# Expert products of split operands in float32r, with the weights split during attention

## What is computed

```python
logits = xf @ Wr / temp
topw, topi = jax.lax.top_k(logits, TOP_K)
topw = jax.nn.softmax(topw, axis=-1)
for e in range(NUM_EXPERTS):
    h = xf @ W1[e] + b1[e]
    a, g = jnp.split(h, 2, axis=-1)
    y = a * jax.nn.silu(g) @ W2[e] + b2[e]
    we = jnp.sum(jnp.where(topi == e, topw, 0.0), axis=-1, keepdims=True)
    out = out + y * we
```

## Time and profile before

| | us |
|---|---|
| median of 3 runs (1123.76 to 1127.93) | 1125.69 |
| the profiled execution | 1125.17 |
| its span, first to last instruction | 1123.4 |
| PE busy | 1019.9 |
| DVE busy | 763.6 |
| ACT busy | 502.1 |
| POOL busy | 409.1 |

### The profile page before, as it was taken

One profiled execution on the slowest core, in us unless ns is written; L12 is line 12 of the kernel. 1 busy time (PEld: TensorE's weight loads), 2 busy tenths in 40 slices (PEclk: granted clock), 3 DMA queues, 4 the chain that ended last, 5 costly groups with the idle time before them and its releaser, 6 DMA issues.

```text
span 1123.4 us, 19233 instructions
## 1 busy us (share of the span) xinstructions
PE 1019.9 (91%) x5236; PEld 525.9 (47%) x5237; DVE 763.6 (68%) x2270; ACT 502.1 (45%) x1060; POOL 409.1 (36%) x777
## 2 busy tenths in 40 slices
PE   5998999999999999999895533999999999999994
PEld 2443233333333333333544531666666666666663
DVE  3776989899999999999464741555555555555552
ACT  2553177777777777777354430221222222222221
POOL 5665333333333333333252673222222222222222
PEclk9998599999999999999897656999999999999998
DMA  2769855556555444417567992222222222323222
GB/s 91 250 220 282 156 124 125 124 127 131 130 131 130 94 95 95 89 42 174 127 205 173 306 310 89 37 45 44 48 47 47 45 44 42 47 47 47 44 45 24
DMA packets 104058, 125.66 MB, mean 112 GB/s; under 512 B 26480, under 2 KB 82416, under 8 KB 103984
## 3 DMA queue, kind: packets, MB, share of 16 engines
q1 hardware_dynamic: 90688, 107.01, 38.5%
q0 software_dynamic: 13296, 17.77, 9.6%
HBM read 74.47 MB, written 49.89 MB: 111 GB/s over the span
## 4 chain that ended last, share of the span: by engine, by line
PE 80%; DVE 6%; POOL 5%; DMA 4%; issue 3%; ACT 2%; SPq 0%; POOLq 0%; DVEq 0%; ACTq 0%
PE bank L1757 22%; PE bank L791 12%; PE bank L812 12%; PE bank L773 12%; PE bank L1774 11%; POOL slot_rows L1169 3%; PE bank L1765 3%; DVE a_xn L314 2%; PE a_ckv L363 1%; PE bank L1745 1%; DVE bank L701 1%; DMA c_heads<-ctx_cols 1%; PE a_k_ps L379 1%; PE bank L1486 1%; DVE b_neg_max L704 1%
## 5 line engine op out<-in xcount | busy, mean ns | idle before, releaser
L747 ACT ACTIVATE b_prob<-bank 128x512 f32<-128x512 f32 (+3 forms) x768 | 311.9, 509 | 79.5 <-PE bank L791 78.6
L773 PE MATMUL bank<-b_k_st,b_q_st 96*128 96x512 bf16 (+3 forms) x768 | 255.5, 346 | 5.8 <-DVE b_neg_max L701 1.7
L1757 PE MATMUL bank<-w_sb,e_rowsT 128*128 x568 | 256.9, 595 | 0.4 <-issue 0.4
L701 DVE CUSTOM_DVE_ANT_0 bank<-bank,b_mask_max 128x256 f32<-128x256 f32 (+3 forms) x512 | 241.5, 508 | 22.9 <-PE bank L773 22.8
L657 POOL TENSOR_SCALAR_AFFINE_SELECT b_prob<-b_prob 128x128 f32<-128x128 f32 x512 | 149.2, 300 | 295.1 <-ACT b_prob L747 290.6
L791 PE MATMUL bank<-b_q_st,b_k_st 99*128 99x512 bf16 (+3 forms) x768 | 242.9, 333 | 4.1 <-ACT b_prob L747 2.0
L1650 POOL DMA_INDIRECT out_dram<-e_y,e_token x71 | 110.5, 1556 | 319.4 <-DVE e_y L1704 294.0
L704 DVE TENSOR_REDUCE b_neg_max<-bank 128x1 f32<-128x512 f32 x256 | 175.7, 686 | 13.7 <-PE bank L773 11.1
L1757 PEld LDWEIGHTS bank<-w_sb,e_rowsT 128*128 128x128 f32 x568 | 102.9, 191 | 103.5 <-issue 103.5
L812 PE MATMUL bank<-b_prob,b_v_aug 128*32 128x512 f32 (+3 forms) x1536 | 146.3, 500 | 0.0
L1774 PE MATMUL bank<-w_sb,e_hiddenT 128*128 x568 | 134.4, 379 | 1.8 <-ACT e_hiddenT L1727 1.8
(11 more groups left out here) (166 smaller groups left out, 886.6 us busy)
## 6 DMA issues: line engine op xcount, KB each, us to landing
w_sb<-in_L_ffn_W SPq DMA_DIRECT2D x12, 1024.0 KB, 5.2
e_rows<-slot_rows SPq DMA_DIRECT2D x72, 129.0 KB, 2.1
ctx_cols<-b_ctx_out SPq DMA_DIRECT2D x16, 512.0 KB
q_parts<-a_part_q SPq DMA_DIRECT2D x8, 768.0 KB, 4.1
k_parts<-a_part_k SPq DMA_DIRECT2D x8, 768.0 KB, 4.8
b_q_st<-q_parts SPq DMA_DIRECT2D x16, 384.0 KB, 4.9
b_k_st<-k_parts SPq DMA_DIRECT2D x16, 384.0 KB, 8.1
a_x<-in_L_attn_x SPq DMA_DIRECT2D x8, 512.0 KB, 5.1
```

The source lines that it names most:

```text
L701: nc.vector.tensor_tensor_reduce(scores, scores, mask_max[:, HALF - width:HALF], -1.0, -MASKED, ALU.add, ALU.min, to).then_inc(max_done, 1)
L747: nc.scalar.activation(prob[n % NP][:, 0:width], prob_ps[n % NS][:, 0:width], ACT.Exp, scale=SCALE).then_inc(prob_ok, 1)
L773: nc.tensor.matmul(out[:, 0:width], q_st[g % RING][0:STACK, h, i * P:(i + 1) * P], k_st[g % RING][0:STACK, h, half * HALF:half * HALF + wi ...
L1757: last = nc.tensor.matmul(out_ps[:], rowsT[c % 2][:, d * P:(d + 1) * P], w1_sb[:, bass.ds(expert, 1), d, first:first + FF].rearrange("p e ...
```

## The change

Each operand of the expert products is written as a high part, rounded to float32r, and a remainder, also float32r. A product becomes three: high by high, high by low, low by high.

- **Weights.** `Weights` holds a ring of 4 slots, each with both parts of one expert's up and down weights (24 KB a partition). During attention SP loads one expert's raw weights (1.5 MB) at `g` = 1, 2, 4, 6, 7, 9, 10, 12, in the order 3, 4, 5, 6, 7, 2, 0, 1. POOL splits each in 12 pieces of 256 columns, a cast and a subtraction a piece, at most one piece a unit. SP stores the parts of the first five (3 MB each) to DRAM at `g` = 4, 6, 8, 9, 11. Experts 2, 0 and 1 stay in SBUF; expert 3 is loaded back in `Route.sync`, in place of the down weights; 4 to 7 are loaded by SP in the expert stage, the up weights when the expert that had the slot has finished its up products, the down weights behind them.
- **Rows and hidden rows.** ACT takes the high part from PSUM (`rows_high`, `hidden_high`), DVE subtracts it for the rest (`rows_rest`, `hidden_rest`).
- **Other moves.** The multiplication by the router's weight goes from DVE to ACT. The load of a tile's rows goes from SP to ACT, behind that multiplication. The second bias is added one step later (`biased`, tile n-3), so there are three steps after the last tile.
- **Adds.** POOL waits for the add two tiles back, and for the last one only where the expert changes (`fresh`, a table that DVE makes), so two adds can be in flight.
- The memory moves follow, and POOL clears `pad_row` when the last context is stored.

```diff
@@ attention, SP @@
-            if 1 <= g <= EXPERTS:
-                sp.dma_start(w1_sb[:, g - 1, :, :], w1[g - 1].rearrange("(c p) n -> p c n", p=P)).then_inc(
-                    loaded, 16)
...
+            if g in W_STORE_AT:
+                weights.store(sp, W_STORE_AT.index(g))
+            if g in W_LOAD_AT:
+                weights.load(sp, W_LOAD_AT.index(g))
@@ attention, POOL @@
+            weights.split_at(pool, unit)
@@ class Weights @@
+    def split(self, pool, k, piece):
...
+        self.nc.gpsimd.tensor_copy(self.ring[:, n, 0, cols], self.raw[:, n, 1, cols]).then_inc(self.high_ok, 1)
+        pool.wait_ge(self.high_ok, k * PIECES + piece + 1)
+        self.nc.gpsimd.tensor_tensor(self.ring[:, n, 1, cols], self.raw[:, n, 1, cols],
+                                     self.ring[:, n, 0, cols].bitcast(F32), ALU.subtract).then_inc(self.split_ok, 1)
@@ experts, SP @@
+        for e in range(W_RING, EXPERTS):
...
+            sp.wait_ge(a_ok, done(e) + 1)
+            weights.load_parts(sp, e, 0)
+            if e == EXPERTS - 1:
...
+                sp.wait_ge(y_ps_ok, done(W_RING) + 1)
+                weights.load_parts(sp, W_RING, 1)
+            sp.wait_ge(weights.parts_in[0], 32 * (e - W_RING + 2))
+            sp.sem_inc(w1_ready, 1)
@@ experts, POOL @@
-            pool.wait_ge(added, (n + 1) * 16)
-            pool.sem_inc(landed, 1)
...
+                pool.wait_ge(added[c % 2], cycle(n, c, 0, 2) * 16)
...
+                pool.wait_ge(added[(c - 1) % 2], cycle(n, c, 1, 2) * 16 + fresh)
@@ experts, ACT @@
+        def load(n, c):
+
+            act.wait_ge(y_ok, n + 1)
...
+            act.dma_start(rows[c % B][:], dram["rows"][bass.ds(row, P), :]).then_inc(rows_ok[c % B], 16)
...
         def step(n, c, value):
+            if value is None or 2 <= n < SLOT_TILES + 2:
+                hidden_high(n - 2, c - 2)
+            if value is None or n + 1 < SLOT_TILES:
+                rows_high(n + 1, c + 1)
+            if value is None or 3 <= n < SLOT_TILES + 3:
+                weighted(n - 3, c - 3)
+            if value is None or n + AHEAD < TABLE:
+                load(n + AHEAD, c + AHEAD)
             if value is None or n < SLOT_TILES:
                 silu(n, c)
-            if value is None or 1 <= n <= SLOT_TILES:
-                hidden_turned(n - 1, c - 1)
@@ experts, PE, up @@
-                    last = nc.tensor.matmul(out_ps[:], rowsT[c % 2][:, d * P:(d + 1) * P],
...
+                    nc.tensor.matmul(out_ps[:], x_hi[:, chunk], moving(slot, 0, at, FF), start=(d == 0), stop=False)
+                    nc.tensor.matmul(out_ps[:], x_hi[:, chunk], moving(slot, 1, at, FF), start=False, stop=False)
+                    last = nc.tensor.matmul(out_ps[:], x_lo[:, chunk], moving(slot, 0, at, FF), start=False,
+                                            stop=(d == DC - 1))
```

More of the change, by code:

```diff
@@ L14 @@
 F32 = mybir.dt.float32
+F32R = mybir.dt.float32r
 BF16 = mybir.dt.bfloat16
@@ L36 @@
 FC = FF // P
-FC_EARLY = 1
 PARTS = 3
@@ L501, in index_of, with attention_phase @@
     return unit // 2 * 2 * QUAD + 2 * h + unit % 2
-def attention_phase(nc, block, life, dram, stacks, projected, room, banks, route, w1, w1_sb, w2, w2_early, loaded):
+def attention_phase(nc, block, life, dram, stacks, projected, room, banks, route, weights):
     NM, NS = 4, 3
@@ L1099, in sync @@
         self.store_x2(sp, 2)
-        for f in range(1, FC):
-            load_w2(f)
+        for layer in range(2):
+            self.weights.load_parts(sp, W_STAGES, layer)
         sp.wait_ge(self.pad_row_ok, 1)
@@ L1555, in tensor, with expert_phase @@
                     self.project(pe, 3, t)
-def expert_phase(nc, block, life, route, dram, room, banks, weights, out):
+def expert_phase(nc, block, life, route, weights, dram, room, banks, bias, loaded, out):
     def sb(name, shape, dt=F32):
@@ L1661, in _ @@
                 add(it * U + c, c)
+        for n in range(2):
+            pool.wait_ge(added[n], (SLOT_TILES - n + 1) // 2 * 16)
     @block.vector
@@ new lines, in build @@
+        weights = Weights(nc, life, low, dram, w1, w2)
+        after = Room(nc, low.next, HIGH)
+        attention = Room(nc, LOW + W_STAGES * 2 * W_COLS * BYTES[F32], HIGH)
+        end = attention.next + ATTENTION_BYTES
+        loaded = life.enter_context(nc.semaphore("loaded"))
+        block = life.enter_context(nc.Block())
+        upper = Room(nc, HIGH - STACKS_BYTES, HIGH)
+        stacks = Stacks(nc, life, upper, dram)
+        freed = Room(nc, upper.first["b_mask_max"], upper.first["b_v_aug0"])
@@ new lines, in build @@
+        over_stacks = Room(nc, upper.first["b_v_aug0"], upper.first["b_ident"])
+        bias = [over_stacks("m_b1", [P, EXPERTS, 2 * FF]), over_stacks("m_b2", [P, EXPERTS, D])]
+        second_row = over_stacks.beside("m_b1", "c_second_row1", [P, BT, ROW])
+        early = Room(nc, end, HIGH - STACKS_BYTES)
+        projected = project_phase(nc, block, life, dram, stacks, Room(nc, LOW, end), x, w_dkv, w_uk, w_uv, w_uq)
+        banks = [life.enter_context(nc.psum_tensor(f"bank{n}", [P, HALF], F32)) for n in range(8)]
@@ new lines, in build @@
+        route = Route(nc, life, early, freed, after, bias, banks, dram, x, w_o, w_r, temp, (b1, b2), weights,
+                      loaded, second_row, out)
+        attention_phase(nc, block, life, dram, stacks, projected, attention, banks, route, weights)
+        assert attention.next <= end and after.next <= end
+        block.sync(route.sync)
+        block.gpsimd(route.gpsimd)
+        block.vector(route.vector)
+        block.scalar(route.scalar)
+        block.tensor(route.tensor)
+        room = Room(nc, upper.first["b_mask_max"], upper.first["b_v_aug0"])
@@ L1841 @@
+        expert_phase(nc, block, life, route, weights, dram, room, banks, bias, loaded, out)
 _INS = ["L0_attn_x", "L0_attn_W_DKV", "L0_attn_W_UK", "L0_attn_W_UV", "L0_attn_W_UQ", "L0_attn_W_O", "L0_ffn_Wr",
```

305 lines of the change are left out of this document (192 added, 113 removed).

## The result

The changed kernel takes **1108.06 us** in the median of 4 runs (1104.23 to 1109.71), the kernel before 1125.87 beside it (1123.76 to 1127.93). The ratio is 0.984, with a 95% interval of 0.9823 to 0.9857. It is faster by 1.6%, clear of the scatter and in the direction of the forecast, but by 18 us where 57 were forecast, and 1108 lies above the range. The profiled execution took 1107.14 us with a span of 1105.4, against 1125.2 and 1123.4 of before.

A forecast was written before the change was run, and what follows sets the result against it. The prediction took PE to bound the expert stage at 5.82 us a step, with the row load's loop next. From 1125.2: -74 for steps, +10 weight loads, +6 attention, +1 tail and start, giving 1068 us; range 1033 to 1105.

The forecast's parts named there:

- d: Expert stage: stationary loads of float32r not hidden at each of 24 products; step 7.1 us, time 1224 us; chance 0.09.
- e: Expert stage: float32r streams at two periods a column; step 8.4 us, time 1315 us; chance 0.05.
- the loop of the row load: Expert stage: row load's loop over two steps, 4.48 plus 5.08 us, sets 4.78 us a step; gain 74 us.
- Reading the expert's number: Expert stage: PE's read of the number between row transposes and products, 0.36 us, taken from the gap at the first tile.
- The products, 0.216 and 0.109: Expert stage: float32r products of 512 and 256 columns at one period a column; PE alone 4.56 us a step.
- rival (b): Expert stage: PE stays the bound at 4.56 us a step, transfers hidden; 1037 us; chance 0.18.
- Rival (c): Transfers cost their upper bounds or the row-load loop is 5.0 us a step; 1093 us; chance 0.17.
- Weight loads in the stage: Expert stage: 12 MB for experts 4 to 7 slows row loads, 9 x 1.1, 10 us; bounds nothing and 27.
- Attention: Attention: SP's queue with the weight stores makes maximum rows late by some 2 us, three times; +6 us, bounds 0 and 15.
- POOL's splits: Attention: 96 pairs of cast and subtraction, 1.2 us each, covered by POOL's waiting; nothing, or 5 to 15 us uncovered.
- The second add, worth nothing at 4.78: Expert stage: one add cycles in 4.7 us, so a second gains nothing at 4.78 us a step, 0.1 at 4.56.
- Tail and start: Ends of the expert stage: tail keeps serial adds (+0.7), first tile gains one remainder; together +1 us.

## Why the prediction was wrong

**The direction and the outline of the mechanism were right.** Float32r streams at about one period a column (0.23 us for 512), the stationary loads stay hidden (rivals d and e fell), PE's own step became short, and what was late next was the row load in a loop over two steps. What failed is the price of a step in that loop: the reading of the expert's number behind the wait for the rows.

**The term that failed: the loop of the row load.** The prediction put 4.48 up to the starts of PE and 5.08 for PE, 4.78 us a step. On the timeline the loop can be read off at its three marks. ACT starts on the hidden rows at 937.65 and issues the row load of line 1839 at 939.68: 2.03, forecast 2.22 (0.60, 0.40, 0.40, 0.82). From that issue to the first up product that it holds up, 943.37: 3.69, forecast 2.80 (landing 2.1, starts 0.12, transposes 0.22, reading 0.36). From there to ACT's next start on hidden rows, 948.27: 4.90, forecast 4.54 (products 3.90, transposes 0.60, start 0.04). Sum 10.62, forecast 9.56; 5.3 a step in place of 4.78.

- *Reading the expert's number, 0.36 of "issue" at the first tile:* this is the main miss, 0.89 of the 1.06 us by which the sum was short. In the loop about 1.6 us pass between the landing and the first product (3.69 less 2.1), where starts, transposes and reading were priced at 0.70. That the order of the two is the cause is shown: with the read moved ahead, the step is 4.86 and the waits are gone. The 0.36 was read as if it were the whole cost. On PE's timeline of the kernel before it is only what stuck out behind the transposes:

```profile
692.43 0.66 PE L1745 MATMUL bank<-m_ident,e_rows 128*128 128x128 f32 x2 [0.68 <-DVE e_rowsT L1672]
```

The first product follows at 693.45. So from the end of the wait to the product it was 1.02 us there (0.66 and 0.36), with the transposes running beside the read, at a granted clock of 0.50; at full clock they take less and hide less. The forecast put 0.58 for the two (0.22 and 0.36); the changed kernel has 1.01 to 1.17 where PE waits for rows.
- *The products, 0.216 and 0.109:* taken from bf16; measured 0.23 and 0.12. They are most of the 0.36 by which the third stretch was short (the first was 0.19 under its forecast). PE alone is 4.86 and not 4.56, so rival (b), 1037, could not have come, whatever was hidden. A fixed address changes nothing in it.

Over 71 steps, (5.29 - 4.78) x 71 = 36 us, most of the 40 missed. The upper bound that the text gave for the loop, 5.3, is what came, but by luck: it stood for landings of 3.2 us, and in the quiet they take 2.1. Rival (c), with a loop of 5.0 or transfers at their upper bounds, gave 1093.

**Weight loads in the stage:** forecast 10, measured 17 (388.1 less 371.4). The mechanism was right, the row load one tile ahead with nothing to spare. The size was off since I took the spread of a quiet stage, landings of at most 3.2. They went to 6.0, near the scatters' 5.2 from which the upper bound was made, and PE's stop brought a second cost that was not in the sum: some 3.2 us at half the clock (where the earlier trace rows show 1.00 in the mean of the stage), which together with the read made the next step 2.5 us longer. The down weights of expert 4 came in time, as forecast. The rule of the Trainium skill ("DMA: Bandwidth & Descriptors", Queues, rings and completion order), which the prediction named as pulling towards the upper bound, agrees in direction with the landings of 6.0; no run tells it from other kinds of contention.

**Attention:** forecast +6, measured 0; the groups are 27.2 apart all through. The stores that were to hold up the maxima did not. The term was placed a group too early (185.3 in place of 211.65), and it was too long: the forecast added 16 us and 12.6 us, which in that group would end 3 us behind the maxima's turn; the transfers ended with it, at 237, and the maxima landed in 1.9 us. POOL's splits at 1.2 us a pair and nothing in all: right.

**The second add, worth nothing at 4.78:** right in the changed kernel (no difference without it, at steps of 5.3). But the rule behind it, that a cycle of 4.7 fits whenever the step is longer, does not hold: with steps of 4.87 it gives nothing, and the cost was some 13 us, because adds beside weight loads take up to 11.2 us and the lag is run off at the end. The text priced the add by its quiet cycle alone.

**Tail and start:** forecast +1, measured 0 (25.4 us both).

The sum with the measured terms: 36 less saved than 74 gives -38, +17 for the loads, 0, 0: -21 against -18 measured. Some 2 of the 3 us left lie in the first three steps, which gained nothing: they take 17.5 us (8.30, 3.51, 5.69) where the kernel before has 17.1 (7.23, 4.09, 5.82).

## What to carry to other kernels

When a step gets shorter, write out the loop of the transfer that now comes late, mark by mark, and count in it what the waiting engine does behind its wait in program order, register reads too: whatever does not need the data belongs ahead of the wait. A row load that runs one step further ahead cost one buffer here and took 45 us off the stage, more than twice what the change itself did, because it covered the quiet loop and the late landings beside weight loads at once. Price an asynchronous operation by its slowest stretch and not by its quiet cycle, if it has little room to catch up.

## What the runs showed of the hardware

Not expected: a float32r product of 512 columns takes 0.23 us and one of 256 columns 0.12, at the full granted clock, some 5 to 9% above the bf16 row of this kernel (0.22) and its half, with a register or a fixed address alike. Float32r stationary loads of 128 columns, 24 a step, are hidden wholly. A register read by PE behind a wait for a semaphore cost some 0.7 us where PE had to wait, left gaps of up to 0.9 us, and cost nothing ahead of the wait. A 129 KB row load took 2.1 us in the quiet and up to 6.0 beside loads of 0.5 to 1 MB. An indirect add landed after 3.8 us in the median and up to 9.1 in the changed kernel; one at a time, the adds start 4.6 us apart, and up to 11.2 beside weight loads. After PE had stood for 2.4 us and, 0.4 us later, for another 0.7, the granted clock was at 0.50 for 3.2 us.
